# One projection moved over a stage border, gates moved by a few steps, and the last tiles handed over in halves

## What is computed

```python
# 1. expert stage: one shared gated layer, 8 routed experts (top 2)
shared = (silu(x @ sw1.T) * (x @ sw3.T)) @ sw2.T
s      = sigmoid(x @ router_w.T + t_emb @ router_t_w.T)      # top 2 -> combine
routed = sum_e combine[:, e] * (gelu(x @ rw1[e].T) @ rw2[e].T)
cond   = (shared + routed) / 3
# 2. selective scan, over each sequence forwards and backwards (4 passes)
u, z   = split(cond @ inproj)
uc     = silu(conv4(u) + conv_b)
dt, B, C = split(uc @ xproj);  delta = softplus(dt @ dt_w + dt_b)
h[t]   = exp(delta[t] * A) * h[t-1] + (delta[t] * uc[t]) * B[t]      # 16 states
y      = (sum_n h * C + uc * D) * silu(z);   out = y @ outproj
# 3. mix: a sigmoid gate weighs the two directions, a projection is added to x,
#    and a threshold picks the tokens of each feature that stay
# 4. soft mixture of 64 linear experts with 32 slots each
dispatch = softmax over tokens, combine = softmax over slots of x @ phi
out      = x1 + combine @ (dispatch.T @ xm @ W[e] + b[e])
```

## Time and profile before

| | us |
|---|---|
| median of 3 runs | 1480.89 |
| lowest and highest | 1474.98, 1485.43 |
| the profiled execution | 1475.89 |
| its span, first to last instruction | 1474.1 |

### The profile page before, as it was taken

One profiled execution on the slowest core, in us unless ns is written; L12 is line 12 of the kernel. 1 busy time (PEld: TensorE's weight loads), 2 busy tenths in 40 slices (PEclk: granted clock), 3 DMA queues, 4 the chain that ended last, 5 costly groups with the idle time before them and its releaser, 6 DMA issues. The chain is left out here.

```text
span 1474.1 us, 14742 instructions
## 1 busy us (share of the span) xinstructions
PE 1185.5 (80%) x4924; PEld 657.9 (45%) x4924; DVE 1148.1 (78%) x1051; ACT 771.5 (52%) x1029; POOL 884.1 (60%) x394
## 2 busy tenths in 40 slices
PE   5999986898639887559887476484598999999998
PEld 3788832232103332113322122131146788787887
DVE  4444458999999999999999999999878654444544
ACT  4444466667645776555775555465256543343330
POOL 4530027999999999999999999999810000000000
PEclk9999998899859998869898677696799999999999
DMA  5344235432363333355123437312015120303011
GB/s 200 107 157 137 93 91 207 157 148 81 141 246 129 115 143 146 107 207 200 71 86 146 161 119 283 142 58 114 12 48 200 35 109 1 143 0 128 0 47 67
DMA packets 46000, 176.34 MB, mean 120 GB/s; under 512 B 5857, under 2 KB 10465, under 8 KB 33522
## 3 DMA queue, kind: packets, MB, share of 16 engines
q1 hardware_dynamic: 45938, 175.57, 32.6%
HBM read 142.78 MB, written 32.77 MB: 119 GB/s over the span
## 5 line engine op out<-in xcount | busy, mean ns | idle before, releaser
L1259 POOL TENSOR_TENSOR scan_dbu<-scan_rep,scan_bc 128x1024 f32<-128x1024 f32 x254 | 592.7, 2364 | 37.4 <-ACT scan_rep L1157 30.1
L1346 DVE TENSOR_TENSOR_SCAN scan_hs<-scan_hs,scan_dbu 128x1024 f32<-128x1024 f32 x191 | 436.7, 2286 | 11.2 <-ACT scan_hs L1184 11.0
L1184 ACT ACTIVATE scan_hs<-scan_rep,scan_neg_a 128x1024 f32<-128x1024 f32 x252 | 280.8, 1118 | 304.8 <-DVE scan_hc L1360 277.3
L1068 PE MATMUL scan_ysum<-scan_hc,scan_sel 128*32 128x512 f32 x1008 | 172.0, 814 | 201.3 <-DVE scan_hc L1360 183.4
L1360 DVE TENSOR_TENSOR scan_hc<-scan_hs,scan_bc 128x1024 f32<-128x1024 f32 x191 | 233.5, 1223 | 6.1
L1068 PEld LDWEIGHTS scan_ysum<-scan_hc,scan_sel 128*32 128x32 f32 x1008 | 35.7, 131 | 317.3 <-issue 269.4
L1265 POOL TENSOR_TENSOR scan_hc<-scan_hc,scan_bc 128x1024 f32<-128x1024 f32 x65 | 153.4, 2360 | 10.1 <-DVE scan_hc L1346 9.9
L1346 DVE TENSOR_TENSOR_SCAN scan_hc<-scan_hs,scan_dbu 128x1024 f32<-128x1024 f32 x65 | 148.1, 2278 | 0.8 <-POOL scan_dbu L1259 0.7
L929 PE MATMUL late_banks<-late_xin,scan_inwf 128*128 128x512 f32 x256 | 116.3, 609 | 0.0
L32 PE MATMUL ffn_sl<-ffn_tanh_s,xm_s 128*128 128x512 f32 x384 | 106.0, 411 | 2.3 <-DVE ffn_tanh_s L2131 2.3
L32 PE MATMUL moe_first<-moe_x_s,moe_w_s 128*128 128x512 f32 x384 | 98.1, 399 | 8.3 <-DVE moe_w_s L436 8.3
(11 more groups left out here) (262 smaller groups left out, 1749.1 us busy)
## 6 DMA issues: line engine op xcount, KB each, us to landing
scan_rep<-dd_rows SPq DMA_DIRECT2D x60, 1024.0 KB, 5.6
scan_bc<-bc_rows SPq DMA_DIRECT2D x32, 512.0 KB, 6.1
ffn_wt<-in_ew SPq DMA_DIRECT2D x16, 1024.0 KB, 7.9
dd_rows<-scan_dd SPq DMA_DIRECT2D x15, 1024.0 KB, 3.8
scan_bc<-gate_rows SPq DMA_DIRECT2D x24, 256.0 KB, 4.8
scan_inwf<-fold SPq DMA_DIRECT2D x12, 512.0 KB, 3.8
cond<-scan_bc SPq DMA_DIRECT2D x16, 256.0 KB, 3.1
y_all<-scan_yo SPq DMA_DIRECT2D x6, 512.0 KB, 3.1
```

What stands on the lines that cost most here:

```text
L1068: mm = nc.tensor.matmul(ysum[i * D32:(i + 1) * D32, h, :], sel[:], hc[:, (s0 + i) % HCR, h * CT:(h + 1) * CT], start=False, stop=last, til ...
L1184: nc.scalar.activation(hs[:, s % HSR, :], rep[:, e % REPS, 0, :], ACT.Exp, scale=scale).then_inc(da_done, 1)
L1259: nc.gpsimd.tensor_tensor(dbu[:, s % DBR, :], rep[:, e % REPS, 1, :], bc[:, j, 0, :], ALU.mult).then_inc(dbu_done, 1)
L1346: nc.vector.tensor_tensor_scan(states, hs[:, s % HSR, :], dbu[:, s % DBR, :], 0.0, ALU.mult, ALU.add).then_inc(scan_done, 1)
```

## The change

Four edits that don't depend on each other.

1. The two PSUM banks of the scan block are taken before the expert block and serve it as the first pair of its ring; `first` shrinks to two pairs. After its last unit TensorE computes `("u", 0, 0, 0)`, the first of the eight first projections, still in the expert block, and `FRONT` starts with the second. The semaphores `bank_ready` move with the banks.
2. In period 0 `gate` comes after `decay` of r = 7 instead of r = 4. The other 15 periods keep 4.
3. The two `first_gate` of period 14 come after r = 9 and 14 instead of 8 and 13.
4. The last eight tiles are handed from TensorE to VectorE by halves: b = 0 always in `oy`, b = 1 in `tb`, a semaphore after each half; VectorE adds and finishes one half before the next. The stores keep their size but for the last tile, which is stored in two halves.

```diff
-        first = ps("first", [P, 3, 2, CT])
+        first = ps("first", [P, 2, 2, CT])
+        ring = [ahead.banks, first[:, 0], first[:, 1]]
...
             project(NC * UNITS - 1)
+            pe.wait_ge(ahead.inwf_in[0], 16)
+            pe.wait_ge(ahead.xin_in[0], 16)
+            for k in range(KC):
+                mm = nc.tensor.matmul(ahead.banks[:, 0, :], ahead.inwf[:, 0, k, 0, :], ahead.xin[0][:, k, TAPS - 1:TAPS - 1 + CT],
+                                      start=(k == 0), stop=(k == KC - 1))
+            mm.then_inc(ahead.bank_ready[0], 1)
...
-GATE_AT = 4
+GATE_AT, FIRST_PERIOD_GATE_AT = 4, 7
...
-FIRST_GATE_AT = {8: 0, 13: 1}
+FIRST_GATE_AT = {9: 0, 14: 1}
...
-            for kind, *args in FRONT:
+            for kind, *args in FRONT[1:]:
...
-                    if r == GATE_AT:
+                    if r == (GATE_AT if w else FIRST_PERIOD_GATE_AT):
...
-            for m in range(MT):
-                sp.wait_ge(res_done, m + 1)
+            for m in range(MT - 1):
+                sp.wait_ge(res_done, BATCH * (m + 1))
                 sp.dma_start(out[:, m * P:(m + 1) * P, :].rearrange("b p d -> p b d"), xres[m]).then_inc(stored, 16)
-            sp.wait_ge(stored, 16 * MT)
+            for b in range(BATCH):
+                sp.wait_ge(res_done, BATCH * (MT - 1) + b + 1)
+                sp.dma_start(out[b, (MT - 1) * P:MT * P, :], xres[MT - 1][:, b, :]).then_inc(stored, 16)
+            sp.wait_ge(stored, 16 * (MT - 1 + BATCH))
...
-                elif last:
-                    pe.wait_ge(acc_done, MT * c + m - 1)
-                else:
+                elif not last:
                     wait(pe, acc_done, MT * c + m)
-                bank = (oy, tb)[m % 2] if last else oy
                 for b in range(BATCH):
+                    if last and m > 0:
+                        pe.wait_ge(acc_done, MT * c + BATCH * m + b - 1)
+                    bank = (oy, tb)[b] if last else oy
...
-                mm.then_inc(out_done, 1)
+                    if last or b == BATCH - 1:
+                        mm.then_inc(out_done, 1)
...
+            def last_output(m, b):
+
+                c, q = NCH - 1, BATCH * m + b
+                dve.wait_ge(out_done, MT * c + q + 1)
+                nc.vector.scalar_tensor_tensor(acc[:, m, b, :], acc[:, m, b, :], alpha[:, c, m, b:b + 1],
+                                               (oy, tb)[b][:, b * DM:(b + 1) * DM], ALU.mult, ALU.add).then_inc(acc_done, 1)
+                dve.wait_ge(acc_done, MT * c + q + 1)
+                nc.vector.scalar_tensor_tensor(xres[m][:, b, :], acc[:, m, b, :], rden[:, m, b:b + 1],
+                                               xres[m][:, b, :], ALU.mult, ALU.add).then_inc(res_done, 1)
...
             for m in range(MT):
-                add_output(NCH - 1, m, last=True)
-                dve.wait_ge(acc_done, MT * (NCH - 1) + m + 1)
                 dve.wait_ge(res_loaded[m], 16)
                 for b in range(BATCH):
-                    last = nc.vector.scalar_tensor_tensor(xres[m][:, b, :], acc[:, m, b, :], rden[:, m, b:b + 1],
-                                                          xres[m][:, b, :], ALU.mult, ALU.add)
-                last.then_inc(res_done, 1)
+                    last_output(m, b)
```

More of the change, by code:

```diff
@@ L124, in moe_phase @@
         by_expert, by_token = second[:, 0, :], second[:, 1, :]
-        t_part, turned = first[:, 2, 1, 0:1], first[:, 1, 1, :]
+        t_part, turned = ring[2][:, 1, 0:1], ring[1][:, 1, :]
         raw, taps_wide = sw1, rw1[:].rearrange("p k (d t c) -> p (k d) t c", d=DC // KC, t=TAPS)
@@ L259, in value @@
                 for k in range(KC):
-                    mm = split_products(nc, first[:, g % 3, 0, :], [w[:, k, u * P:(u + 1) * P] for w in w1_s],
+                    mm = split_products(nc, ring[g % 3][:, 0, :], [w[:, k, u * P:(u + 1) * P] for w in w1_s],
                                         [x[:, k, c * CT:(c + 1) * CT] for x in x_s], k == 0, k == KC - 1)
@@ L274, in factor @@
                 wait(pe, hid_split, g - 2)
-                out = first[:, g % 3, 1, :]
+                out = ring[g % 3][:, 1, :]
                 if u < SU:
@@ L351, in hidden @@
                 wait(act, hid_done, g - 1)
-                nc.scalar.activation(act_h[:, g % 2, :], first[:, g % 3, 0, :], ACT.Silu if g % UNITS < SU else ACT.Gelu
+                nc.scalar.activation(act_h[:, g % 2, :], ring[g % 3][:, 0, :], ACT.Silu if g % UNITS < SU else ACT.Gelu
                                      ).then_inc(act_done, 1)
@@ L362, in high_hidden @@
                     act.wait_ge(hid_used, (UNITS - 1) * c + u + 1)
-                nc.scalar.activation(hid_s[0][:, g % HB, :], first[:, g % 3, 1, :], ACT.Copy).then_inc(hid_high, 1)
+                nc.scalar.activation(hid_s[0][:, g % HB, :], ring[g % 3][:, 1, :], ACT.Copy).then_inc(hid_high, 1)
             def output(c):
@@ L445, in product @@
                     dve.wait_ge(factor_done, FACTORS[g])
-                    other = first[:, g % 3, 1, :]
+                    other = ring[g % 3][:, 1, :]
                 dve.wait_ge(act_done, g + 1)
-                nc.vector.tensor_tensor(first[:, g % 3, 1, :], act_h[:, g % 2, :], other, ALU.mult).then_inc(hid_done, 1)
+                nc.vector.tensor_tensor(ring[g % 3][:, 1, :], act_h[:, g % 2, :], other, ALU.mult).then_inc(hid_done, 1)
             def low_hidden(g):
                 dve.wait_ge(hid_high, g + 1)
-                nc.vector.tensor_tensor(hid_s[1][:, g % HB, :], first[:, g % 3, 1, :], hid_s[0][:, g % HB, :].bitcast(F32),
+                nc.vector.tensor_tensor(hid_s[1][:, g % HB, :], ring[g % 3][:, 1, :], hid_s[0][:, g % HB, :].bitcast(F32),
                                         ALU.subtract).then_inc(hid_split, 1)
@@ L630, in __init__ @@
         self.bc = sb("bc", [P, NJ, 2, SEQ])
+        self.banks = ctx.enter_context(nc.psum_tensor("scan_banks", [P, 2, CT], F32))
+        self.bank_ready = [ctx.enter_context(nc.semaphore(f"scan_bank_ready{i}")) for i in range(2)]
         self.stored = [[ctx.enter_context(nc.semaphore(f"scan_stored{d}_{cc}")) for cc in range(KC)] for d in range(2)]
@@ L663, in __init__ @@
         first.xin.append(sb("xin1", [P, KC, TAPS - 1 + SEQ]))
-        self.banks = ctx.enter_context(nc.psum_tensor("late_banks", [P, 2, CT], F32))
+        self.banks = first.banks
         self.gb, self.prb, self.rv = sb("gb", [P, KC]), sb("prb", [P, KC]), sb("rv", [P, KC, BATCH])
@@ L723, in mamba_phase @@
             "consts_in", "zeroed", "neg_done", "diag_done"))
-        bank_ready = [sem(f"bank_ready{i}") for i in range(2)]
+        bank_ready = ahead.bank_ready
         bank_free = [sem(f"bank_free{i}") for i in range(2)]
@@ L2093, in turn_out, with add_output @@
                                       ).then_inc(et_dve, 1)
-            def add_output(c, m, last=False):
+            def add_output(c, m):
                 dve.wait_ge(out_done, MT * c + m + 1)
                 dve.wait_ge(alpha_done, MT * c + m + 1)
-                bank = (oy, tb)[m % 2] if last else oy
                 for b in range(BATCH):
                     step = nc.vector.scalar_tensor_tensor(acc[:, m, b, :], acc[:, m, b, :], alpha[:, bass.ds(c, 1), m, b],
-                                                          bank[:, b * DM:(b + 1) * DM], ALU.mult, ALU.add)
+                                                          oy[:, b * DM:(b + 1) * DM], ALU.mult, ALU.add)
                 step.then_inc(acc_done, 1)
+            def last_output(m, b):
[6 more added lines that the diff above has]
+                                               xres[m][:, b, :], ALU.mult, ALU.add).then_inc(res_done, 1)
             def chunk(c, first=False, final=False):
```

## The result

| | before | after |
|---|---|---|
| median, us | 1482.99 (22 runs, 1474.98 to 1485.85) | 1476.63 (22 runs, 1471.57 to 1480.19) |
| ratio of after to before | | 0.9963, 95% interval 0.9951 to 0.9975 |
| the profiled execution | 1475.89 | 1476.72 |
| its span | 1474.1 | 1474.9 |

The change saves 5.5 us by the ratio, 6.0 by the means (1481.56 and 1475.58; two standard errors are 1.8). The forecast was 4.64 saved and 1474.7 us; it put before at 1479.3, and 22 runs put it at a median of 1482.99. But the two profiled executions show no gain: after's span is 0.8 us longer.

A forecast was written before the change was run, and what follows sets the result against it. No engine is busy throughout, so the bound changes by block, with VectorE pacing the scan block. Terms 0.87 + 1.74 + 1.03 + 1.00 = 4.64 us, taken from a mean of 1479.3, gave 1474.7 us, range 1469 to 1481.

The forecast's parts named there:

- Edit 1: Border and front: the early projection fits before SyncE's last issue and removes ScalarE's wait behind its table load, −0.87 us.
- wrong if the second block begins after 187.2: Test at the border after the expert block: a second block beginning after 187.2 us would refute the projection-ahead term.
- Edit 2: Period 0: moving the gate removes ScalarE's 2.87 us stall at scan 5; GpSimd at scan 10 leaves −1.74 us.
- Edit 3: Period 14: stalls of 2.18 and 0.55 become about 0.5 each; VectorE gains 1.7 us, GpSimd's end leaves −1.03.
- Edit 4: Last block: one half instead of a tile behind TensorE's end, −0.80 us, and a smaller last store, −0.2.
- Sum: All four edits: 0.87 + 1.74 + 1.03 + 1.00 = 4.64 us saved; chance of all as summed 0.62.
- GpSimd took 1.1 of edit 2: Rival in the scan block: GpSimd takes the scan's gains, the sum falls to 2.2 us, time 1477.1; chance 0.17.
- The table switch costs its load: Rival at period 0's gate: each switch costs more than its load, that term falls to 0.9, time 1475.5; chance 0.03.
- The slower case, TensorE's clock after the new pause: Rival in the front: clock at 1.2 GHz after the second projection adds up to 10.7 us, time 1485.4; chance 0.04.
- Span shrinks by 2 to 7: Test on the whole execution: the forecast is wrong if the span shrinks by less than 2 or more than 7 us.
- the border in front of the last block moves by 3.6: Test at the last block's start: the forecast is wrong if that border moves by anything but 3.6 us.

The follow-up runs named there:

- e10: The changed kernel with GpSimd's two chores of period 0 moved to r = 10 and 11; median 1476.24 us, ratio to before 0.9954.
- e1: The kernel before with only the projection ahead of the border added; median 1476.47 us, ratio to before 0.9971.
- e3: The kernel before with only the two first gates of period 14 moved to r = 9 and 14; median 1481.68 us, ratio to before 0.9996.
- e5: The changed kernel run once more, nothing altered; median 1473.13 us, ratio to before 0.9956.
- e6: The changed kernel with period 14's first gates at r = 10 and 15, and the gate of periods 3, 7, 11, 15 at r = 6; 1476.09 us, ratio to before 0.9970.
- e2: The kernel before with only the gate of period 0 moved to r = 7; median 1479.72 us, ratio to before 0.9992.
- e11: The kernel before, unchanged, in a further profiled execution; 1483.91 us.
- e4: The kernel before with only the last tiles handed over in halves; median 1477.74 us, ratio to before 0.9985.
- e8: The changed kernel with the projection of each period's gate computed twice; one execution, 1517.49 us.
- e9: The changed kernel with the projection ahead of the border computed twice; one execution, 1478.73 us.

## Why the prediction was right, step by step

**Edit 1, −0.87.** Right in place, order and size: ScalarE's 0.90 is gone, 0.9 to 1.3 between executions at like clock. The test "wrong if the second block begins after 187.2" was badly put and failed on its letter (187.63): that border moves by 1.3 us from one execution of unedited code to the next. The gap behind SyncE, 0.40, was the thing to name.

**Edit 2, −1.74.** 1.70 to 1.73, with the stall at scan 10 (1.07 to 1.09, "about 1.1") for the very reason given; e10 took it away. Not seen was that 1.71 of the 2.94 us was the clock in the gate's projection, so that edit 2 alone brings 1.7 or nothing, by that clock (e1).

**Edit 3, −1.03.** The step that failed is one reading: the stall of 2.18 at 987.37 was taken as fixed. Its larger part, the 1.41 behind L1026, is there in two of five executions. The arithmetic on it held (stalls 0.55 and 0.55 for "near 0.5"; 1.65 on VectorE for "1.7"; GpSimd as the bound in e3 and e5). So the term is 1.0 in one kind of execution and nothing in the other.

**Edit 4, −1.00.** About 1.2. VectorE's part was 0.78 for 0.80. The term that was mis-sized is the store, 0.4 for 0.2: I took the price of 128 KB from a transfer of another kind in the earlier trace rows (1.9), and the halves themselves take 1.7. The Trainium skill ("DMA: Bandwidth & Descriptors", section "Anatomy of one DMA — SWDGE (gpsimd) path") has 2.0 us plus bytes over 436e3, which gives an estimate of 0.30 for 128 KB less. It is a fit to transfers that GpSimd issues; these are SyncE's, and the 0.4 measured is above it as well.

**Sum.** By the traces 1.1 + 1.7 + (0 or 1.0) + 1.2: 4.0 to 5.0, for 4.64 forecast and 6.0 ± 1.8 measured. The edits one by one add up to −7.6 ± 5.8. That the sum comes out near 4.64 is in part luck: edit 3's term is right in two of five executions, more than half of edit 2's stall rests on a clock that happened to be low there in all five executions without edit 1, and the excess of edits 1 and 4 makes up for some of it. What more is in the 6.0 goes with the share of runs at the high clock, which the prediction has no term for.

**The rivals.** GpSimd took 1.1 of edit 2, and 0.6 of edit 3 in e3 and e5, as summed, not more. The table switch costs its load. The slower case, TensorE's clock after the new pause: from 187 to 200 the granted clock was 1.00 in all eight traces with edit 1, so it didn't come. (The 0.86 from 200 to 224 came with and without the edit.)

**The tests.** "Span shrinks by 2 to 7" and "the border in front of the last block moves by 3.6" were both missed, by a span 0.8 longer and a border 0.5 later (1126.5 for 1126.0), though the forecast of the median held. A test on one pair of executions has to be on lengths between neighbouring instructions. The span of one moves by 8 us with no edit.

## What to carry to other kernels

Price a stall only after asking what else must be late for it: where an engine's wait ends on a TensorE group, compare that group's duration with its duration at full granted clock, and count only the rest as the kernel's own. An edit worth one to two microseconds is to be looked for as the length between two fixed instructions, in two or more executions of each kernel. And before the profiled executions stand for the kernel, compare their clock and time with those of all runs: here the changed kernel's 15 runs at 0.901 or more have no trace among them. And where two engines share a bound, moving one of them pays what the other leaves: VectorE ended the scan block 4.7 us earlier in e6 than in e5, and the mix began 3.65 earlier (1062.79 for 1066.44), as GpSimd kept the rest.

## What was not expected of the hardware

- The eight records of a gate's projection take 3.60 to 3.71 us at full clock and up to 5.94, by the granted clock of the stretch: in period 11 3.70 in e2 (1.00), 4.16 in before (0.88), 5.93 in e11 (0.62). Before, e11 and e2 run the same code there. In a block that VectorE bounds, with TensorE busy 71 to 72% of it from 240 to 960, this goes with a spread of the executions: before lay between 1474.8 and 1485.9 us in 35 runs.
- The low level comes after a pause of TensorE, but not each time: after the pauses from 1120 to 1135 (6.75 us of records in the ten to 1130) the granted clock stayed at 1.00 in before, and fell to 0.83 in after (1130 to 1140). It is the 376.6 or 378.2 us of the mix and the last block: before, e4 and e8 had 1.00 there and 376.6, e11 had 0.95 and 378.2, and e1, e2, e3, e5, e9, e10 and after had 0.83 and 378.2.
